# A graph-attention kernel: VectorE's operations of an edge group in another order, with the additions of sums behind the guard

## The reference: what is computed

```python
q, k, v = heads(xp @ Wq + bq), heads(xp @ Wk + bk), heads(xp @ Wv + bv)
att = einsum('ehd,ehd->eh', q[dst], k[src]) / scale
att = nan_to_num(clip(att, -50.0, 50.0), nan=0.0)
ex = exp(att - segment_max(att, dst)[dst])
alpha = ex / (segment_sum(ex, dst)[dst] + 1e-16)
aggr = segment_sum(v[src] * alpha[:, :, None], dst)
x = x + (aggr @ Wo + bo)
x = x + (gelu(layernorm(x) @ W1 + b1) @ W2 + b2)
```

## Time and profile before

| | |
|---|---|
| time, median of 3 runs | 2185.11 us (2184.74 to 2186.89) |
| span of the profiled execution | 2183.8 us, 1.3 us under the median |
| GpSimd busy | 1570.6 us (72%), of it gathers 1530.7 |
| VectorE busy | 1710.2 us (78%) |
| TensorE busy | 1419.8 us (65%) |
| ScalarE busy | 940.2 us (43%) |

### The profile page before, as it was taken

How to read it: one execution, slowest core, us unless ns; L and a number is a source line. 1 busy time by engine, 2 the same in 40 slices (tenths; PEclk the granted TensorE clock), 3 DMA queues, 4 the chain that set the end, 5 groups by cost and what they waited for, 6 DMA issues and landing times.

```text
span 2183.8 us, 32409 instructions
## 1 busy us (share of the span) xinstructions
PE 1419.8 (65%) x8227; PEld 1237.3 (57%) x8227; DVE 1710.2 (78%) x5103; ACT 940.2 (43%) x2179; POOL 1570.6 (72%) x1669
## 2 busy tenths in 40 slices
PE   4866576666667676766666657566666757666666
PEld 4555565656555565655556556556555656555555
DVE  8759888888877878787877777777777778777775
ACT  8334353534535353534454335343343435343344
POOL 6277777777777777777727777777777777777773
PEclk9979888877878788887988787787787778787787
DMA  2365445444444444444424444444444444444441
GB/s 87 119 178 182 148 133 154 147 136 134 142 134 125 142 134 142 124 142 134 132 69 143 135 125 136 137 123 139 133 139 124 139 134 129 134 134 138 125 138 56
DMA packets 123505, 289.29 MB, mean 132 GB/s; under 512 B 31525, under 2 KB 57057, under 8 KB 123329
## 3 DMA queue, kind: packets, MB, share of 16 engines
q0 software_dynamic: 77824, 212.31, 33.8%
q1 hardware_dynamic: 45504, 74.92, 10.3%
HBM read 275.44 MB, written 8.38 MB: 130 GB/s over the span
## 4 chain that ended last, share of the span: by engine, by line
POOL 47%; issue 20%; DVE 11%; PE 11%; DMA 6%; ACT 3%; DVEq 1%; SPq 0%; ACTq 0%
POOL kvr L801 47%; DMA kvr<-kv_table,srcidx 5%; PE bank L1079 4%; PE bank L1092 3%; DVE agg L1706 3%; DVE kvr L1322 2%; DVE prod L1675 1%; DVE msg L1697 1%; ACT apart L1279 1%; ACT onehotT L1283 1%; DVE onehot L1667 1%; PE bank L1036 1%; PE bank L1015 1%; PE bank L816 1%; PE bank L894 1%
## 5 line engine op out<-in xcount | busy, mean ns | idle before, releaser
L801 POOL DMA_INDIRECT kvr<-kv_table,srcidx x1612 | 1530.7, 950 | 547.4 <-issue 480.0
L1079 PE MATMUL bank<-q,onehotT 128*128 x3320 | 606.8, 340 | 712.1 <-DVE prod L1675 475.2
L1079 PEld LDWEIGHTS bank<-q,onehotT 128*128 128x128 f32 x3320 | 515.6, 237 | 825.5 <-issue 824.8
L1092 PE MATMUL bank<-msg,onehot 128*128 128x136 f32 x3320 | 612.3, 344 | 1.9 <-DVE msg L1697 1.9
L1289 ACT ACTIVATE bank<-attc 128x32 f32<-128x32 f32 x404 | 81.2, 201 | 1145.7 <-DVE attc L1691 1145.0
L1092 PEld LDWEIGHTS bank<-msg,onehot 128*128 128x128 f32 x3320 | 571.8, 252 | 3.6 <-DVE msg L1697 3.3
L1675 DVE TENSOR_TENSOR prod<-kvr,bank 128x512 f32<-128x512 f32 x404 | 276.0, 683 | 302.6 <-DMA kvr<-kv_table,srcidx 264.0
L1706 DVE TENSOR_TENSOR agg<-agg,bank 128x136 f32 x1624 | 469.1, 289 | 44.9 <-PE bank L1092 40.1
L1279 ACT ACTIVATE apart<-relT,minus_p 128x512 bf16<-128x512 bf16 x416 | 293.8, 706 | 4.4 <-DMA relT<-rel_table 4.0
L1667 DVE TENSOR_TENSOR onehot<-bank,rel 128x512 f32<-128x512 f32 x416 | 282.5, 682 | 0.2
L1697 DVE TENSOR_TENSOR msg<-kvr,bank 128x512 f32<-128x512 f32 x404 | 273.9, 678 | 5.0 <-ACT bank L1289 4.9
(11 more groups left out here) (217 smaller groups left out, 844.5 us busy)
## 6 DMA issues: line engine op xcount, KB each, us to landing
relT<-rel_table SPq DMA_DIRECT2D x104, 512.0 KB, 4.1
kvr<-kv_table,srcidx POOLq DMA_INDIRECT x1612
loop_kv<-kv_table SPq DMA_DIRECT2D x25, 128.0 KB, 3.9
kv_table<-qkv SPq DMA_DIRECT2D x25, 128.0 KB, 3.2
kv_table<-onehot SPq DMA_DIRECT2D x8, 256.0 KB, 2.2
w<-weights SPq DMA_DIRECT2D x2, 840.0 KB, 7.4
loops<-x_in SPq DMA_DIRECT2D x5, 320.0 KB, 5.6
q<-qkv SPq DMA_DIRECT2D x25, 64.0 KB
```

Of the source, the lines that this page charges most:

```text
L801: pool.indirect_dma_start(kvr[:, n % RING, j, :], None, kv_table[l], bass.IndirectOffsetOnAxis(ap=srcidx[:, step:step + 1], axis=0)).then_ ...
L1079: mm = pe.matmul(bank[2][:, j * D:(j + 1) * D], onehotT[:, m % OHT, j, :], q[:, bass.ds(ranks[j + h], 1), :].rearrange("p a c -> p (a c)") ...
L1092: mm = pe.matmul(sum_ps(n, k), onehot[:, m % OH, j, :], msg[:, n % 2, j, :], start=(m, j) == of[0], stop=(m, j) == of[-1])
```

## The change

The same instructions, in another order within `edge_iteration`. Before, an addition stood behind the product, the message, the scores and the clip, and the one-hots ahead of the guard. Now the message stands right behind the product, the one-hots right behind the scores, the first addition between clip and guard, and the other three (four in a seam) behind the guard, at the end of the iteration. The change also takes blank lines off the head of the file, so each line of the program has a number smaller by 16.

```diff
                 edge_prod(n)
-                add(0)
                 if g >= 1:
                     edge_msg(n - 1)
-                add(1)
                 edge_att(n)
-                add(2)
+                if g + 2 < GROUPS:
+                    edge_onehot(n + 2)
                 edge_clip(n)
-                add(3)
+                add(0)
+                edge_guard(n)
+                for j in range(1, G):
+                    add(j)
                 if g >= 2 and is_seam(n - 2):
                     add(G)
-                if g + 2 < GROUPS:
-                    edge_onehot(n + 2)
-                edge_guard(n)
```

## The result

Measured side by side, the changed kernel takes 2216.0 us (median of 4 runs, 2209.6 to 2219.1) against 2185.9: ratio 1.0134, 95% interval 1.0117 to 1.0151, 30 us slower. The profiled execution has a span of 2217.4 us, 33.6 more than that of before; it belongs to the longest of the four runs (2219.1 us).

What follows compares the result with a forecast made beforehand. GpSimd's gathers, 1.25 us apart, were taken to bound the kernel. VectorE would end layer 0 26 us late and layer 1 2 us late: 2185.1 + 28 = 2213 us, 1.3% slower, range 2195 to 2236.

Steps and rivals of the forecast that it cites:

- the added work: VectorE in layer 0: 0.87 us more per plain iteration, 0.61 per dense one, 153.7 us in all.
- the relief in the dense waits: Layer 0: dense work starts later, so waits less for TensorE; 34 of 44.0 us taken off, bounds 17 and 44.
- Additions in a chain: End of a VectorE iteration: dependent additions start 0.44 us apart, against 0.21 with another instruction between.
- The load, no longer hidden: VectorE's queue ahead of each product: block-number load comes behind the held last addition, about 0.47 us to product, not 0.21.
- A plain iteration: VectorE, product to product without dense work: 4.41 us instead of 3.54, 0.87 more.
- What gets free: Layer 0's waits for TensorE: 21.9 us back at the first additions, 34 us in dense pieces.
- the signs of being wrong: In the new trace: additions at 0.21, load starting ahead of the last addition, or dense waits staying as they are.
- Layer 1 free but for its end: Layer 1: about 129 us net fits under 188.0 us of gather waits; only the end costs, 2 us (1 to 4).
- Where the lateness shows: GpSimd's gap between the layers: about 22 to 26 us longer than 34.7, less lateness moved by the full ring.
- hidden after all: Rival: additions at 0.21 or an overlapping load, VectorE keeps up with the gathers, 2185 to 2189 us; 8%.
- faster: Rival: waits for TensorE that go outweigh the chain, layers' ends gain 4.4 us, 2180.7 us; 4%.
- Harder: Rival: dense waits hardly shrink (17) or new ones arise, layer 0 late by 43 or more, 2230 to 2240 us; 10%.

Runs made afterwards that it cites:

- experiment 1: Changed kernel with the load of the next block numbers moved behind the scores, ahead of the one-hots, additions still chained: 2182.3 us, ratio 0.9990.
- experiment 4: Kernel before, old order, with a wait for the guard's end put ahead of the load of the next block numbers: 2184.6 us, ratio 1.0004.
- experiment 2: Changed kernel's order in layer 1 alone, the old order in layer 0: 2184.6 us, ratio 0.9999.
- experiment 7: Changed kernel's order in layer 0 alone, the old order in layer 1: 2210.1 us, ratio 1.0113.
- experiment 6: Changed kernel with one addition put back between message and scores, two left behind the guard, load still behind them: 2183.3 us, ratio 0.9996.
- experiment 5: Changed kernel with a wait for the last addition's end put ahead of the load of the next block numbers: 2245.1 us, ratio 1.0266.

## Why the prediction was right

Forecast 2213 us, measured 2216; as a change, 28 and 30 us. The mechanism was the one described. That the size came out so close is luck: two terms of the sum, the added work and the relief in the dense waits, were both some 20 us too large and cancel. With only the work put right the sum of layer 0 would have been 8 us, with only the relief put right 48.

- *Additions in a chain, 0.44 us:* right to the digit. These additions stand 0.44 us apart dependent and next to each other, and 0.21 with another instruction between them. The Trainium skill, VectorE: DVE Perf Modes, section "The DRAIN you can't avoid", measures chained copies as equally long with a semaphore after each and with one at the end; for these additions the trace disagrees. How the 0.23 divides can be read from the self-loop scores of the dense work, where each operation also waits by semaphore for the one before, but with no register instruction between:

```profile
356.57 0.18 DVE L1574 TENSOR_TENSOR loop_nan<-loop_att 128x24 uint8<-128x24 f32 x1
356.78 0.18 DVE L1575 TENSOR_SCALAR loop_att<-loop_att 128x24 f32<-128x24 f32 x1
```

  The second starts 0.03 us behind the end of the first (the median of all 72 such pairs too). The same two operations in an edge iteration, without a wait between them, start 0.08 ahead of that end (175.13 and 175.23 above), and a chained addition starts 0.15 behind the end of the one before (0.44 less 0.29). So some 0.11 us goes with the wait and 0.12 with the register instruction behind it; this compares different operations, and no run takes the register instruction out.
- *The load, no longer hidden:* right: 0.47 us from last addition to product. Experiments 1 and 4 show it from both sides.
- *A plain iteration* takes 4.37 us; the sum had 4.41. Addition 0 starts 0.08 behind the second of clip's operations, not 0.12. Counted product to product, without waits for gathers, sums and dense pieces, the 119 plain iterations of layer 0 became 93.6 us longer (104.9 forecast, seams included) and the 80 dense ones 46.1 (52.8 with the 4 us put back). Work was over-priced by 18 us.
- *What gets free:* the 21.9 us of the first additions went entirely. The dense waits did not: 44.0 us became 32.5, so 11.5 went where I had taken 34. With the other execution of either order (51.0 in experiment 2, 33.3 in experiment 7) it is 11 to 19 us: at best about my lower bound of 17. This is the mis-sized step, and of the signs of being wrong that the prediction names, dense waits that stay as they are came nearest. The sum with the measured terms is 93.6 + 46.1 - 21.9 - 11.5 - 76.0 = 30 us, and the last product of layer 0 starts 30.9 us later behind the first one than before; the two must agree, since the terms are that stretch itself, sorted.
- *Why the dense waits stayed.* Half of the argument held: TensorE does wait less for the transposed one-hots. TensorE's query products in layer 0, before (L1079) and after (L1063): busy, mean ns, idle before and its causes:

```profile
L1079 PE MATMUL bank<-q,onehotT 128*128 x1644 | 293.2, 334 | 342.2 <-DVE prod L1675 206.1 <-ACT onehotT L1283 136.0
...
L1063 PE MATMUL bank<-q,onehotT 128*128 x1644 | 309.5, 347 | 340.8 <-DVE prod L1659 320.9 <-ACT onehotT L1267 19.9
```

  The wait for ScalarE fell from 136.0 to 19.9 us, and nearly all of it turned into waiting for VectorE's product. TensorE is idle as long as before, and its products take longer, 347 ns for 334. The granted clock over layer 0 is 0.79 where it was 0.82 (rows before and after; behind stretch and length a row has busy time and number of instructions of PE, PEld, DVE, ACT and POOL, then the granted clock, DMA share and GB/s):

```profile
125.10:1116.30 991.20, 648.90 (x3737) 566.24 (x3738) 821.73 (x2515) 434.41 (x958) 744.90 (x785) 0.82 0.47 141
127.10:1149.30 1022.20, 681.45 (x3738) 599.15 (x3739) 870.90 (x2515) 436.78 (x958) 744.69 (x784) 0.79 0.46 137
```

  A dense piece where it shows, group 46 of the changed kernel, from product over query product to the piece that waits, and the windows row of that stretch:

```profile
357.47 0.69 DVE L1659 TENSOR_TENSOR prod<-kvr,bank 128x512 f32<-128x512 f32 x1 [0.28 <-issue]
...
358.40 2.07 PE L1063 MATMUL bank<-q,onehotT 128*128 x8 [3.58 <-DVE prod L1659]
...
364.33 0.61 DVE L1551 SCALAR_TENSOR_TENSOR qkv<-u_deg,deg,bank 128x384 f32<-128x384 f32 x1 [2.69 <-PE bank L974]
...
358.30:362.20 3.90, 3.80 (x16) 3.57 (x16) 3.03 (x10) 1.59 (x4) 2.88 (x4) 0.50 0.37 101
```

  TensorE has been idle for 3.58 us, is granted 0.50, the 1.2 GHz level, and its eight products take 2.07 us; the median group takes 1.15. They take over 1.6 us in 78 of the 195 groups of layer 0 that have eight of them, before in 56. In the kernel before, group 46 has the same idle time, at 0.65 its products take 1.87 us, and the piece waits 2.13 instead of 2.69:

```profile
341.44 1.87 PE L1079 MATMUL bank<-q,onehotT 128*128 x8 [3.58 <-DVE prod L1675]
```

  Counted in the timelines, 29 iterations of layer 0 have a dense piece that waits for TensorE, 44.0 us before and 32.4 after (the 32.5 above adds rounded rows). They fall into three sorts by what TensorE does in the changed kernel. In 12 the granted clock is 0.90 or less from query product to waiting piece (in 5 of them before): 20.7 us before, 22.2 after, nothing gained. In six, all of one kind (L1020), the clock is full, but the query product starts some 2.3 us behind VectorE's product, before 1.3 to 2.3: 8.9 us and 7.9. There the premise that TensorE starts no later failed. In the other 11, 14.4 us became 2.3, as the prediction had argued. So the relief that is missing is missing where the clock is low or the query product late; that the low clock is the cause in the 12 is argued from these rows, not tested by a run.
- *Layer 1 free but for its end:* right. From its first gather to the end it is 0.9 us longer, where 1 to 4 were forecast, and experiment 2 loses nothing. But it used 96 us of its waits where the sum had 129. Where a product still waits for its gather, the load runs within that wait and its price isn't paid: 112 such waits at 0.47 - 0.21 = 0.26 are 29 us, an estimate that nearly covers the 33.
- *Where the lateness shows:* GpSimd's gap between the layers grew by 23.7 us, within the 22 to 26 forecast, and some 6 us had already moved into waits on the full ring.
- *The rivals:* "hidden after all" is what experiments 1 and 6 make true, with either price taken out. Of the "faster" one there is at most 0.2% of the time in experiment 1. "Harder" has its first half, dense waits that hardly shrink, but not its price, since the work was smaller than forecast.

## What to carry to other kernels

What an engine that isn't the bottleneck can be charged is the time in which it waits for the bottleneck, stage by stage: here 76 us in one layer and 188 in the other, nothing to be seen up to that, and most of the price beyond (29 of 37 us in experiment 5). Two prices that are each free can lose together, so the test of one alone proves little. Keep short dependent operations apart by independent ones, and put work that the instruction queue does itself, such as loading registers, ahead of long operations and not behind an instruction that holds the queue.

## What the runs showed of the hardware that I had not expected

TensorE released sooner was not done sooner: with the wait for its one-hots cut from 136.0 to 19.9 us in layer 0, it waited as long in all for another engine (342.2 and 340.8 us), and at a granted clock of 0.79 instead of 0.82 its query products took 347 ns instead of 334.

On VectorE a semaphore between two operations had a price even without a register instruction: two small operations without a wait started 0.10 us apart, the same two with one 0.21.
